# A two-layer decoder on one core: 22 warming products at the ternary layer's entry, and twelve more between its convolution taps

## What is computed

```
x = x + windowed_attention(layernorm(x))                 # 64-wide blocks, one head of 256
x = x + latent_attention(ctx, layernorm(x))              # 8 heads of 128, 1536 keys
x = x + ternary_ffn(layernorm(x))                        # the part that is changed here
x = x + self_attention(layernorm(x))                     # 16 heads of 16
x = x + cross_attention(layernorm(x), ctx)               # 16 heads of 16, rotary
x = x + routed_ffn(layernorm(x))                         # 8 experts, the best one is taken
```

```
h = quantised(x) @ ternary(w1).T          # 256 -> 1024 hidden channels
h = conv_w[0]*h[t-1] + conv_w[1]*h[t] + conv_w[2]*h[t+1] + conv_b   # three taps along the tokens
h = silu(h)
out = quantised(h) @ ternary(w2).T        # 1024 -> 256
```

## Time and profile before

| | |
|---|---|
| median of 3 executions | 2151.58 us (2150.91 to 2153.02) |
| the profiled execution's own time | 2151.76 us |
| its span, first to last instruction | 2150.0 us |
| TensorE busy | 1959.8 us, 91% |
| VectorE busy | 1720.8 us, 80% |
| ScalarE busy | 1310.5 us, 61% |
| GpSimd busy | 263.6 us, 12% |
| mean granted TensorE clock | 0.993 of full speed |

### The profile page before, as it was taken

How to read it: one execution, slowest core, us unless ns; L and a number is a source line. 1 busy time by engine, 2 the same in 40 slices (tenths; PEclk the granted TensorE clock), 3 DMA queues, 4 the chain that set the end, 5 groups by cost and what they waited for, 6 DMA issues and landing times.

```text
span 2150.0 us, 42930 instructions
## 1 busy us (share of the span) xinstructions
PE 1959.8 (91%) x17894; PEld 1108.1 (52%) x17894; DVE 1720.8 (80%) x2681; ACT 1310.5 (61%) x1953; POOL 263.6 (12%) x280
## 2 busy tenths in 40 slices
PE   1999988989999998889999999898999999889898
PEld 0577753323657774242466777333256777533235
DVE  7788878696888887879588888869868888786956
ACT  3566646578356664638636665574944666556682
POOL 2000001242000000135000000103500000011430
PEclk9999999999999999999999999999999999999999
DMA  6166630020036661003005666002101666400200
GB/s 273 38 126 126 128 85 13 9 94 24 18 77 131 123 141 40 13 10 113 11 21 111 123 126 141 8 6 78 45 11 42 126 126 126 101 12 9 94 2 11
DMA packets 424210, 156.39 MB, mean 73 GB/s; under 512 B 405928, under 2 KB 416560, under 8 KB 423120
## 3 DMA queue, kind: packets, MB, share of 16 engines
q1 hardware_dynamic: 423440, 151.54, 29.7%
q0 software_dynamic: 576, 2.10, 0.3%
HBM read 43.43 MB, written 2.16 MB: 21 GB/s over the span
## 4 chain that ended last, share of the span: by engine, by line
PE 62%; DVE 27%; ACT 5%; issue 3%; DMA 2%; POOL 0%; SPq 0%; POOLq 0%; DVEq 0%; ACTq 0%
DVE nmx L2012 14%; PE ps L654 11%; PE ps L656 11%; PE ps L655 11%; PE ps L1022 6%; PE ps L816 4%; PE ps L810 3%; PE ps L811 3%; PE ps L1008 3%; DMA arena<-arena 2%; PE ps L972 1%; DVE st L1656 1%; DVE arena L1824 1%; PE ps L1032 1%; PE ps L1089 1%
## 5 line engine op out<-in xcount | busy, mean ns | idle before, releaser
L2012 DVE TENSOR_REDUCE nmx<-ps 128x2 f32<-128x1024 f32 x384 | 444.6, 1218 | 14.6 <-PE ps L972 13.0
L1519 ACT ACTIVATE arena<-ps 128x512 f32<-128x512 f32 x768 | 406.1, 600 | 49.7 <-PE ps L1008 44.9
L654 PE MATMUL ps<-arena 128*128 128x512 f16 (+1 forms) x784 | 266.6, 340 | 1.3 <-DVE arena L1748 1.1
L655 PE MATMUL ps<-arena 128*128 128x512 f16 (+1 forms) x784 | 266.5, 340 | 0.0
L656 PE MATMUL ps<-arena 128*128 128x512 f16 (+1 forms) x784 | 266.5, 340 | 0.0
L1811 DVE TENSOR_SCALAR_CACHE_REDUCE ps<-ps 128x1536 f32<-128x1536 f32 x128 | 225.7, 1764 | 40.5 <-PE ps L656 39.9
L1022 PE MATMUL ps<-arena 128*17 128x256 f32 x3072 | 240.4, 389 | 0.0
L1824 DVE SCALAR_TENSOR_TENSOR arena<-arena,rs 128x1536 f16<-128x1536 f32 x128 | 231.6, 1810 | 4.2 <-ACT arena L1413 4.2
L1413 ACT ACTIVATE arena<-arena,rs 128x1536 f16<-128x1536 f32 x128 | 200.8, 1569 | 42.9 <-DVE rs L1817 42.9
L1406 ACT ACTIVATE arena<-ps,nm 128x1536 f32<-128x1536 f32 x128 | 197.1, 1540 | 8.3 <-DVE ps L1811 8.3
L626 POOL TENSOR_TENSOR rstd<-ve,col 128x2 f32<-128x2 f32 x40 | 29.3, 732 | 1284.8 <-DVE ve L1917 864.4
(11 more groups left out here) (285 smaller groups left out, 3733.1 us busy)
## 6 DMA issues: line engine op xcount, KB each, us to landing
arena<-in_experts SPq DMA_DIRECT2D x4, 3840.0 KB, 11.5
arena<-in_weights SPq DMA_DIRECT2D x8, 929.0 KB, 12.4
arena<-arena SPq DMA_DIRECT2D x72, 64.0 KB, 2.1
arena<-in_ctx SPq DMA_DIRECT2D x4, 1024.0 KB, 5.7
arena<-arena SPq DMA_TRANSPOSE x256, 3.2
arena<-in_ctx_t SPq DMA_DIRECT2D x4, 1024.0 KB, 4.9
arena<-arena SPq DMA_DIRECT2D x72, 32.0 KB, 1.9
arena<-in_ternary SPq DMA_DIRECT2D x2, 1024.0 KB, 5.8
```

Source lines behind the costliest of these rows:

```text
L654: mm(out_, lh, rh, start=(k == 0), stop=False)
L655: mm(out_, lh, rl_, start=False, stop=False)
L1519: A(pr_[:, n % RING, :], ps[:, 4 + n % 3, :], ACT.Exp).then_inc(b_exp.sem, 1)
L2012: V.tensor_reduce(nmx[:, g_ % 2, ch, :, pp, i], ps[:, 2 * (z % 2):2 * (z % 2) + 2, :], AX.X, ALU.max, negate=True)\
```

## The change

Three places in `bitnet(b)` on TensorE change; nothing changes on the other engines.

- At the entry TensorE waits for the batch's last exponential instead of the second `xo_added`, and runs 22 warming products instead of 16.
- In the loop over blocks, four warming products into bank 5 stand behind block 3's products, ahead of its `early_transposes(0)`.
- Behind the loop TensorE waits for the fifth `h_conv` (which frees bank 2, block 4's), and runs four warming products into bank 2 ahead of `early_transposes(5)` and four ahead of `early_transposes(6)`.

That is 18 more products in a batch, and 72 in the program.

```diff
             def bitnet(b):
-                pe.wait_ge(xo_added.sem, xo_added.at(b, 2))
-                keep_warm(16, 4)
+                pe.wait_ge(s_exp.sem, s_exp.at(b, NT * XH))
+                keep_warm(22, 4)
                 transpose_y(b, 1)
...
                     last.then_inc(h_mm.sem, 1)
+                    if m == 3:
+                        keep_warm(4, 5)
                     if m >= 3:
                         early_transposes(m - 3)
+                pe.wait_ge(h_conv.sem, h_conv.at(b, HB + 1))
                 for m in range(NM - 3, NM):
+                    if m < NM - 1:
+                        keep_warm(4, H_BANK[0])
                     early_transposes(m)
                 pe.wait_ge(h_conv.sem, h_conv.at(b, NM))
```

## The result

The changed kernel took 2156.16 us (median of 10 executions, 2153.95 to 2159.35), the kernel before 2152.15 us (10 executions, 2149.14 to 2155.99): a ratio of 1.0022, 95% interval 1.0013 to 1.0030. It is slower by 4.0 us where 0.6 us less was forecast, and it lies above the stated range. (A ratio here is an estimate with its interval from all executions of both kernels, so it differs a little from the quotient of the medians.) The profiled execution took 2157.97 us, its span is 2156.2 us; it lies 1.8 us above its kernel's median, so what follows accounts for the 6.2 us between the two profiled spans and not for the 4.0 us between the medians.

A forecast was written before the change was run, and what follows sets the result against it. TensorE, busy 91% of the span and 62% of the last-ending chain, was the bound. Entry 0, block 3 taps 0 and last-tap falls -0.6 us gave 2151.2 us for the profiled execution, 2151.0 us as median; range 2148.4 to 2153.3 us.

The forecast's parts named there:

- The new instructions hide: Entry and taps: all added warming products fit TensorE's idle time at full clock; if none hid, 15.7 us in all.
- The last taps' falls go, 1.22 us at the stage's end: Last taps, batches 0 and 1: filling the thin stretch removes the clock's falls, 0.61 us each.
- The entry gains nothing: Ternary layer's entry: earlier start and 22 products taken as 0, bounds 1.09 us gained or lost per batch.
- Half of the 1.22 us is kept: Behind the stage, self attention onward: half of the last taps' gain survives, -0.6 us in the total.
- rival 2: Falls only move or the self attention gives the gain back: 2151.6 us, up to 2152.4 us; chance 0.25.
- Entry 0, taps at block 3 0: Terms of the sum: the entry's part and the four products behind block 3 each change the time by 0.
- A scatter of 1.85 us that dwarfs the gain: From L1048 to the next batch's L1903: 479.20, 477.49 and 479.34 us for the same instructions, taken as scatter.
- what I overlooked: Whole kernel: unforeseen part of the 15.7 us upper bound; with rival 3 it made slower by 0.2%, chance 0.04.
- Rival 3: Entry: warming products meet half clock, 3.9 us late each batch; two batches give 2159.3 us; chance 0.03.

The follow-up runs named there:

- e7: The kernel before with only the entry's part (earlier start, 22 warming products) and small filler products holding the instruction blocks; 2149.28 us, ratio 0.9989.
- e5b: Repeat of e5, the kernel before with 33, 29 and 33 products of 8 columns in batches 0, 1 and 2; 2149.67 us, ratio 0.9990.
- e4b: Repeat of e4, the changed kernel with small products holding the instruction blocks; 2149.89 us, ratio 0.9991 to the kernel before.
- e6: The changed kernel with its entry undone, only the products between the taps, small products holding the instruction blocks; 2149.68 us, ratio 0.9991 to the kernel before.
- e1: The kernel before with 18 products of 8 columns per batch at the ternary layer's entry, no warming added; 2158.94 us, ratio 1.0027.
- e4: The changed kernel with 15, 11 and 15 products of 8 columns in batches 0, 1 and 2; 2150.16 us, ratio 0.9988 to the kernel before.
- e8: e5 with 18 instead of 33 small products in batch 2; 2153.66 us, ratio 1.0008 to the kernel before.
- e0: The changed kernel run again without any edit; 2157.70 us, ratio 1.0021 to the kernel before.
- e5: The kernel before with 33, 29 and 33 products of 8 columns in batches 0, 1 and 2; 2148.23 us, ratio 0.9982.

## Why the prediction was wrong, point by point

- **The new instructions hide**: right for their own length. Each group ended ahead of the instruction behind it, and y's transposes start 8.17 us behind the first addition (8.16 us before).
- **The last taps' falls go, 1.22 us at the stage's end**: right. No batch with the products had one, and the four stages are 1.2 us shorter in the two profiled executions, 1.3 us in the means of thirteen (about 1.0 us of that by 11 of 28 falls of 0.6 us, the rest by fewer falls at the entry). The sum behind it was loose: it put all eight products into the stretch of 3.40 us, which most of the first four precede. The same stretch after, 312.92 to 316.32 us, was busy for 2.83 us and not 3.18.
- **The entry gains nothing**: borne out; falls there occur with and without it, and e7 equals e5b within 0.4 us. That each of the two profiled executions had just one, in batch 2 and then in batch 3, was luck.
- **Half of the 1.22 us is kept**: not borne out. With the blocks held, e4b and e6 are not below e5b, and the means above have 1.3 us less in the stage and 1.6 us more behind it. That it is given back in the attentions, rival 2's case, fits these means, but the single executions' sums behind it scatter by more (803.5 to 808.4 us), so it is not shown.
- **"Entry 0, taps at block 3 0"**: this step of the sum failed. Time was priced, place was not. The 36 instructions per batch moved TensorE's instruction blocks by 36, 72 and 108 against the latent attention of batches 1 to 3, and with them the DMA transposes that they met: 5.1 us in the latent stages and 1.1 us at the load of batch 2's x, in the profiled execution. e1 reproduces this without the change, e4 removes it with the change in place, and e8 moves it to another batch.
- **"A scatter of 1.85 us that dwarfs the gain"**: the evidence was there and was misread. The 479.20, 477.49 and 479.34 us are not mere scatter: the latent stages in them, 192.41, 190.82 and 192.60 us, are places 66, 132 and 198, and place 132 stayed the shortest in all 14 stages that have it. Some scatter is left within a place: 204, next to 198, gave 192.78 us in the kernel after, but 191.70 and 191.92 in e0 and e1. Stretches that repeat the same instructions and differ by 1.8 us ask for the reason.
- **The chances**: slower by over 0.2% had 0.04, "what I overlooked", and was priced by the length of the products. Rival 3 was a clock rival; in none of the 52 batches did the warming products of the entry meet a granted clock of 0.50. The time came out slower than the range for a reason that no rival had.

## What to carry to other kernels

In this unrolled program every TensorE instruction added or removed moves the block edges of all its later code, and where TensorE waits for DMAs that leave little slack, this alone was worth 4 to 6 us (e8 against e5b, the changed kernel against e4), more than the edit. Other engines' instructions were not tried. Before a small edit is judged, count the instructions that it adds per repeated stage and compare the stage's copies with each other; and judge it with the blocks held at the same places, by small products in idle time, as e4b to e7 do. A version found in passing, the kernel before with 95 small products (e5, e5b: 0.9982 and 0.9990 of its time, intervals up to 0.9990 and 0.9999), beats both kernels by a little; the warming adds nothing to it that can be measured.

## What the runs showed of the hardware

- One 16,384-byte instruction packet among a pair of DMA transposes goes with 4.2 to 5.1 us to landing instead of 3.2 us (twelve transposes at six such places), and with 2.1 to 2.6 us for the issue of the second one of the pair instead of 1.4 us. A latent stage has 17 packets (one has 16) and only one to four waits of TensorE for a DMA of over 0.1 us, so most packets cost nothing.
- A fixed program has such waits at fixed instructions, to 0.1 us in distance over separate executions (174.5 and 22.8 or 22.9 us), while their sizes vary, one by 0.3 us and one by 1.0 us, and each kernel's set of executions spreads over 4 us and more.
- TensorE's fall to 1.2 GHz is a matter of the execution as well as of the work: at the last taps 11 of 28 like batches had it, and with eight products, some 1.7 us, in the idle time none of 24.
